# Reading the edge lists and making the chunk tables inside layer 0's front, instead of at the head of the adjacency stage

## The reference, cut to what matters

```python
xn = _layernorm(x, axis=-1)
agg = jax.ops.segment_sum(x[src], dst, num_segments=n)   # inside gin_conv, twice, with src and dst swapped
h = (1.0 + eps) * x + agg
q, k = elu(x @ Wq) + 1, elu(x @ Wk) + 1                  # inside the mix
x = x + gnn(xn, edge_index, ...) + mix(xn[None], ...)[0]
x = x + ffn(_layernorm(x, axis=-1)[None], ...)[0]
```

## Time and profile before

| | |
|---|---|
| median of 3 runs | 2361.12 us (2360.05 to 2365.64) |
| profiled execution, its own time | 2366.88 us |
| its span, first to last instruction | 2365.1 us |
| mean granted TensorE clock | 0.907 of full speed |
| busy: PE, PE weight loads, DVE, ACT, POOL | 1997.1, 1624.9, 1474.2, 1036.3, 551.5 us |

### The profile page before, as it was taken

The page is one execution under the profiler, slowest core; times in us unless marked ns, Lnnn a source line. Parts: engine busy times, 40 slices in busy tenths (PEclk is TensorE's granted clock), DMA queues, the critical chain, the costliest instruction groups (busy, mean ns, idle before and its releaser), DMA issues. The chain is left out here.

```text
span 2365.1 us, 41463 instructions
## 1 busy us (share of the span) xinstructions
PE 1997.1 (84%) x12047; PEld 1624.9 (69%) x12047; DVE 1474.2 (62%) x3791; ACT 1036.3 (44%) x1835; POOL 551.5 (23%) x612
## 2 busy tenths in 40 slices
PE   6938888878877758998697898769999965999998
PEld 3526666656633447998365776569888854999997
DVE  3479999978832655554565322399999656444443
ACT  3525555545511524665351343166666430333332
POOL 1000000047611734554310000000000001454443
PEclk9979999977898559999798999989999956999999
DMA  2014334330077301221502342212121081633332
GB/s 69 0 46 133 117 121 129 109 93 1 1 168 211 103 25 54 71 71 54 127 0 54 95 136 63 56 42 65 53 66 53 0 291 54 195 79 75 49 47 33
DMA packets 90653, 189.74 MB, mean 80 GB/s; under 512 B 14121, under 2 KB 58432, under 8 KB 90570
## 3 DMA queue, kind: packets, MB, share of 16 engines
q1 hardware_dynamic: 72906, 157.31, 23.0%
q0 software_dynamic: 17664, 31.47, 6.4%
HBM read 124.22 MB, written 64.52 MB: 80 GB/s over the span
## 5 line engine op out<-in xcount | busy, mean ns | idle before, releaser
L2224 PEld LDWEIGHTS experts_ps_h<-experts_xt,experts_up 128*128 128x128 f32 x2944 | 351.8, 194 | 10.3 <-issue 3.3
L2224 PE MATMUL experts_ps_h<-experts_xt,experts_up 128*128 128x128 f32 x2944 | 353.0, 277 | 3.0 <-DVE experts_xt L2346 1.8
L2851 PE MATMUL gat_ps_o<-Y,gat_prob_t 125*125 125x256 f32 x1250 | 273.9, 379 | 0.0
L2851 PEld LDWEIGHTS gat_ps_o<-Y,gat_prob_t 125*125 125x125 f32 x1250 | 232.7, 188 | 33.7
L1233 PE MATMUL adj_ps_w<-adj_one_k,adj_one_s 128*125 128x500 bf16 x1000 | 178.8, 305 | 78.6 <-DVE adj_one_k L1164 56.0
L2236 PE MATMUL experts_ps_o<-experts_down,experts_hid 128*128 128x256 f32 x960 | 226.7, 379 | 0.0
L2284 ACT ACTIVATE experts_down<-down 128x1024 f32 (+1 forms) x120 | 138.8, 1157 | 175.7 <-DVE experts_out L2334 77.1
L2316 DVE COPY experts_up<-up 128x1024 f32 (+1 forms) x184 | 123.1, 698 | 112.8 <-issue 68.8
L1233 PEld LDWEIGHTS adj_ps_w<-adj_one_k,adj_one_s 128*125 128x125 bf16 x1000 | 98.3, 138 | 128.6 <-DVE adj_one_k L1164 60.2
L2236 PEld LDWEIGHTS experts_ps_o<-experts_down,experts_hid 128*128 128x128 f32 x960 | 173.2, 190 | 18.7
L1177 ACT ACTIVATE adj_tile<-adj_ps_w 125x500 bf16<-125x500 f32 x250 | 95.8, 438 | 150.1 <-PE adj_ps_w L1233 150.1
(11 more groups left out here) (436 smaller groups left out, 3783.9 us busy)
## 6 DMA issues: line engine op xcount, KB each, us to landing
adjacency<-adj_tile SPq DMA_DIRECT2D x25, 683.6 KB
adjacency_t<-adj_tile_t SPq DMA_DIRECT2D x25, 683.6 KB
adj_in<-adjacency_t SPq DMA_DIRECT2D x25, 683.6 KB
QT<-adjacency SPq DMA_DIRECT2D x25, 683.6 KB
cnt<-adjacency_t SPq DMA_DIRECT2D x25, 683.6 KB
up<-in_L_ffn_w SPq DMA_DIRECT2D x32, 512.0 KB, 6.3
down<-in_L_ffn_w SPq DMA_DIRECT2D x16, 512.0 KB, 7.1
up<-in_L_ffn_W SPq DMA_DIRECT2D x8, 512.0 KB, 6.2
```

The lines of the kernel that those rows point to most:

```text
L2224: last = nc.tensor.matmul(ps[:, h * 128:(h + 1) * 128], w[:, k * H + h * 128:k * H + (h + 1) * 128], xt[b][:, k, :], start=(k == 0), stop= ...
L2851: last = nc.tensor.matmul(ps_o[b][0:ROWS, 0:C], prob_t[:, s * ROWS:(s + 1) * ROWS], K.Y[:, s, :], start=(s == 0), stop=(s == TILES - 1))
```

## The change

The tiles of the lists and tables, and the code that makes them, move from `build_adjacency` into a class `Edges`. Its tiles are allocated ahead of `front`'s and stay through both stages (`MixDown`'s weights are now allocated ahead of them too). `front` of layer 0 calls the pieces: SP loads the three lists behind the rows of group 1 and ahead of `wq`; POOL writes the number rows first, and runs the all-reduce behind the copy of group 3 (`GROUPS - 2`); DVE does seven portions between the tiles of its groups. DVE's and POOL's loops over groups become straight code there. `build_adjacency` keeps the windows alone. `front` of layer 1 has no `edges` and is as it was.

```diff
-def front(nc, K, stage, w_y, y_width, w_kv, w_q, y_scale, x_from=None, x_landed=None, next_sems=0):
+def front(nc, K, stage, w_y, y_width, w_kv, w_q, y_scale, x_from=None, x_landed=None, next_sems=0, edges=None):
...
             rows(1)
+            if edges is not None:
+                edges.load(sp, K.D)
             sp.dma_start(wq[:], w_q.rearrange("(k p) o -> p k o", p=128)).then_inc(w_in, 16)
...
                     if u < 2:
                         then(u)
+                    if edges is not None:
+                        if (g, u) == (0, 3):
+                            edges.widen(dve)
+                        if (g, u) == (1, 2):
+                            edges.halves(dve)
+                        if (g, u) == (1, 3):
+                            edges.keys(dve)
+                        if (g, u) == (2, 2):
+                            edges.presence(dve)
+                        if (g, u) == (2, 3):
+                            edges.spans(dve)
+                        if (g, u) == (3, 3):
+                            edges.bounds(dve)
+                        if (g, u) == (4, 1):
+                            edges.chunks(dve)
...
-            if x_from is not None:
-                with pool.Fori(0, GROUPS) as g:
+            if edges is not None:
+                edges.numbers()
+                for g in range(GROUPS):
                     save(g)
+                    if g == GROUPS - 2:
+                        edges.spread_spans(pool)
...
+    def spread_spans(self, pool):
+        pool.wait_ge(self.span_ready, 1)
+        self.nc.gpsimd.partition_all_reduce(self.span_all[:].rearrange("p a q w -> p (a q w)"),
...
+    def halves(self, dve):
+        v = self.nc.vector
+        v.tensor_scalar(self.off[:], self.src_f[:], 0.5, 1.0 / ROWS, ALU.add, ALU.mult)
+        v.tensor_reduce(self.least[:], self.dst_rows[:], AX.X, ALU.min)
+        dve.drain()
+        v.tensor_copy(self.hi_i[:], self.off[:])
+        v.tensor_reduce(self.most[:], self.dst_rows[:], AX.X, ALU.max)
+        dve.drain()
+        v.tensor_copy(self.hi[:], self.hi_i[:])
+        dve.drain()
...
+    def bounds(self, dve):
+        dve.wait_ge(self.spread, 1)
+        self.nc.vector.tensor_reduce(self.ends[:], self.span_all[0:1].rearrange("p a q w -> p a w q"), AX.X, ALU.max)
+        dve.drain()
```

More of the change, by code:

```diff
@@ L374, in group @@
                 last.then_inc(q_used, 1)
-            overlapped(dve, GROUPS, (statistics, normalise), group)
+            if edges is None:
+                overlapped(dve, GROUPS, (statistics, normalise), group)
+            else:
+                statistics(0, 0)
+                normalise(0, 0)
+                for g in range(GROUPS - 1):
+                    group(g, g % 2, lambda k: (statistics, normalise)[k](g + 1, (g + 1) % 2))
+                group(GROUPS - 1, 0, lambda k: None)
             dve.wait_ge(sum_done, 1 + START)
@@ L967, in build_adjacency @@
         m = Memory(nc, st, "adj", K.banks)
[L968 to L992, removed]
+        E = K.edges
+        low_all, key_all, key_row, win_key, table = E.low_all, E.key_all, E.key_row, E.win_key, E.table
         one_s = [m.sb(f"one_s{i}", (CH, FIXED, ROWS), BF16) for i in range(2)]
@@ L1111, in _ @@
-            v.tensor_reduce(most[:], dst_rows[:], AX.X, ALU.max)
-            dve.wait_ge(made, 1 + START)
-            v.tensor_scalar(rank_up[:], chunk_no[:], 1.0, None, ALU.add)
-            v.tensor_scalar(rank_down[:], chunk_no[:], -1.0, float(CHUNK_ROWS), ALU.mult, ALU.add)
-            dve.drain()
-            for q in range(4):
-                v.tensor_scalar(here[:, q, :], win_first[:], float(WIN - 1), least[:, q:q + 1], ALU.add, ALU.is_ge)
-                v.tensor_scalar(here2[:, q, :], win_first[:], most[:, q:q + 1], None, ALU.is_le)
@@ L1119, in _ @@
-            dve.drain()
-            v.tensor_tensor(here[:], here[:], here2[:], ALU.mult)
-            dve.drain()
-            for q in range(4):
-                v.tensor_scalar(span[:, 0, q, :], here[:, q, :], rank_up[:, q:q + 1], None, ALU.mult)
-                last = v.tensor_scalar(span[:, 1, q, :], here[:, q, :], rank_down[:, q:q + 1], None, ALU.mult)
-            last.then_inc(span_ready, 1)
-            dve.wait_ge(spread, 1 + START)
-            v.tensor_reduce(ends[:], span_all[0:1].rearrange("p a q w -> p a w q"), AX.X, ALU.max)
@@ L1128, in _ @@
-            dve.drain()
-            v.tensor_scalar(row[:, 0, :], ends[:, 1, :], -1.0, float(CHUNK_ROWS), ALU.mult, ALU.add)
-            dve.drain()
-            v.tensor_scalar(row[:, 0, :], row[:, 0, :], float(CHUNKS), None, ALU.min)
-            dve.drain()
-            v.tensor_tensor(row[:, 1, :], ends[:, 0, :], row[:, 0, :], ALU.subtract)
-            dve.drain()
-            v.tensor_copy(table[:, 0:WINS], row[:, 0, :])
-            v.tensor_reduce(most_chunks[:], row[:, 1, :], AX.X, ALU.max)
@@ L2896, in program @@
                     K.QT = sb(conv, "QT0", (128, KC, NODES))
[L2897 to L2898 removed]
                     K.md = MixDown(nc, conv, D)
[L2900 removed]
+                    with ExitStack() as listed:
+                        K.edges = Edges(nc, listed, K.banks)
+                        front(nc, K, "front0", D["L0_gnn_W1_down"], 64, D["L0_mix_Wkv"], D["L0_mix_Wq"], None, D["x"],
+                              next_sems=ADJ_SEMS, edges=K.edges)
+                        build_adjacency(nc, K, D)
                     K.X1 = K.XN
```

137 lines of the change are left out of this document (90 added, 47 removed).

## The result

The changed kernel takes a median of 2341.3 us (2338.24 to 2343.33, 4 runs) against 2361.78 of the kernel before (2360.05 to 2365.64, 4 runs). The ratio on record, from the fast runs, is 0.9907, with an interval from 0.9889 to 0.9926; the two medians by themselves give 0.9913. The forecast was 2341. So the time is right, and so is the large term. Of the small terms three are off, and they offset each other only in part; most of what follows is about these.

A forecast was written before the change was run, and what follows sets the result against it. PE bounds the front, table making alone fills the gap before the windows, and DVE bounds the windows. -23.4 + 3.0 + 0.3 = -20.1 us on the profiled 2366.88 gives 2346.8, a median of about 2341; range 2334 to 2349.

The forecast's parts named there:

- the large term: Between front and first window: table making leaves the path, first window at 130.32 instead of 153.76, -23.4 us.
- The gap: From the front's last DVE copy to the first window: 2.5 us instead of 25.9, so -23.4 us.
- The portions: DVE in the front: 14.9 us of table work over five groups, all hidden in DVE's waits.
- portions not hidden: Rival, DVE in the front: a closer chain through PE and ACT puts 14.9 us back, 2356; chance 0.06.
- The lists: Front's start: 692 KB of transfers ahead of `wq` delay PE's first transposes and the whole front, +3.0 us.
- The queue is full, so the case is nearest the full-share rows: Transfers ahead of `wq`: step choosing +3.0 us, with 217 GB/s giving 3.2 and bounds 0 to 5.2.
- One port: POOL and DVE in the front hold each other up at `halves` or `QT`: 0 to 3.5 us, taken as +0.3.
- POOL's change of code: POOL in group 3, ahead of the all-reduce: 7.2 us, leaving 9.5 us to spare before `bounds`.
- rival on a long change: POOL's code change is long and `bounds` holds the front; slower by over 0.3% from 49 us, 2372 at 60; chance 0.02.
- The entry into the windows: Start of the adjacency stage: taken as free; the rival prices hidden DVE entry at 0 to 5.2 us, chance 0.07.
- The windows at the same pace: Adjacency stage: sign that the windows still take 320 us.
- if a later stage gives time back: Stages behind the adjacency stage: one of the signs that the prediction is wrong.

The follow-up runs named there:

- hold: The changed kernel, but POOL's copy of the normalised rows waits for tile 2's key of the group before; median 2340.74 us, ratio 0.9895 to the kernel before.
- lists: Lists read early as in the changed kernel, but all tables made at the adjacency stage's start and POOL's copies in a loop; median 2360.37 us, ratio 0.9985.
- loop: The changed kernel, but POOL's copies of groups 0 to 3 stand in a loop again, with no new wait; ratio 0.9906.
- shift53: The changed kernel with lists behind all front rows, POOL's copy waiting for tile 2's key, and 53 one-element DVE memsets in the front; ratio 0.9897.
- unrolled: The kernel before, with POOL's loop over its five copies written out and nothing else; ratio 0.9991.

## Why the prediction came out right

**The gap** (-23.4 us) was right to 0.1: the work of the earlier trace rows is gone from the path, and the entry of 2.5 us is all that is left.

**The portions** were hidden, as forecast, in the idle time of DVE that the earlier trace rows shows: the same front of 107.14 us with them (`hold`) and without (`lists`). The working for group 1 was near (tile 3's key by 59.4 at the old times; 60.27 + 0.41 - 0.56 - 0.61 = 59.5 measured, taking off the later start and the 0.61 lost in group 0). The rival "portions not hidden" is refuted.

**The lists** (+3.0 us) were mis-sized: 1.9 us over twelve kernels. The step that failed is "The queue is full, so the case is nearest the full-share rows": a full share was read as a fixed rate, 217 GB/s, while the queue moves up to 348 at the same share, and moved 331 in the old trace. A profile pair is also too little for such a term, since the first transposes scatter by 1.2 to 1.6 us among kernels of one kind.

**One port** (+0.3 us) was mis-sized and put in the wrong place. The forecast looked for new work beside POOL, at `halves` and at `QT`. In the changed kernel neither pair meets: `halves` starts at 57.60, after the copy's end at 57.40, and `QT` at 89.74, after the all-reduce's at 86.84. With the copy behind the key, which the forecast took for granted, the hold-up at `halves` is of the size forecast: `loop` has it, at 0.30 us. The port cost 3.44 us at an old pair, the key of tile 2 and POOL's copy, which the earlier trace rows shows 0.13 us apart, in the order that is good for PE. The forecast named neither that distance nor what writing out both loops does to it. The 3.44 lie just within the stated bound of 3.5. DVE's code without a loop gives 1.05 back, which was not forecast either, so the front grew by 2.39. The Trainium skill, SBUF — State Buffer, "Who interferes with whom", says that whoever issues first gets the shared ports for the whole instruction and the other waits, and that a TENSOR_REDUCE never contends. The trace agrees for POOL's copy: 1.48 us for the key behind a copy of 1.25, 1.40 to 1.52 for the copy behind a key of 0.41, and 0.68 for the reduction beside the copy in `hold`. It doesn't for the all-reduce: the CAST that starts 0.12 us behind it ends at 85.68, 1.16 us ahead of it, and lost 1.59 us, not the 3.11 that were left of it (the spans of such POOL instructions are rough).

**POOL's change of code** was forecast at 7.2 us and took less. In the ten kernels in which the spans are ready before it is over, the all-reduce starts 5.55 to 5.94 us after POOL's last instruction; in the other four it starts 0.14 us after the last span. `bounds` went as forecast, without a wait at 98.87. In the rival on a long change the 2372 is a slip: from slower by 0.3% (2368) at 49 us, each further us lost, 60 us give 2379.

**The entry into the windows** was free, as forecast: in `lists` DVE begins 0.29 us after the front's end. No run shows DVE's entry to be a branch that stalls for a fetch.

**The windows at the same pace** was wrong by 1.8 us, a term the forecast did not have.

In the profiled pair the terms add up to the end of the adjacency stage: -23.46 + 0.56 + 2.39 + 1.82 = -18.69. With 1.9 for the lists it would be -17.4, where -20.1 was forecast and the medians show -20.5. So the forecast was closer than its terms, and that it met the median within 0.3 us is in part luck: it had 1.1 us too much for the lists, 2.1 too little for the port and 1.8 too little for the windows, 2.8 too little in all.

The other 2 or 3 us are not explained. The forecast named "if a later stage gives time back" as a sign of being wrong, and in the profiled pair the stages behind do: from the next stage's first instruction to the end they take 1870.3 us in place of 1880.3. But they are the same code in all fourteen kernels, and in the eleven with the portions in the front they take from 1870.3 (changed) to 1881.2 us (`shift53`), 1875.5 on the mean; `unrolled` takes 1879.8, `lists` 1875.1. So these single executions can't tell a gain of a few us behind from scatter. The interval of the ratio, 17.5 to 26.2 us, leaves it open too.

## What to carry to other kernels

Work that doesn't depend on its neighbours can be put into the idle time of a busy stage at no cost, if it is cut into portions smaller than each idle stretch; read those stretches from the waits of the engine that gets the work, and the wants of the engine that waits for it. But writing out a loop to make room for such portions shifts every instruction in it by hundredths of a microsecond, and where two engines share a port, look up in the old trace which pairs start close to each other (0.13 us here): there such a shift can turn the order, and one wait on the right semaphore fixes it. Put transfers that are needed late behind those that hold the start.

## What was not expected of the hardware

- A distance of 0.05 us decides who has the port: POOL's copy 0.05 us ahead of the key costs PE 0.94 us in groups 1 to 3 (0.61 in group 0), and a copy 0.01 us behind the key costs it nothing.
- Straight code is not simply sooner than a loop: POOL's copy starts 0.06 us after its rows in place of 0.18, DVE's key 0.11 in place of 0.05.
- The transfers moved 209 to 348 GB/s at a share of 1.03 to 1.07.
- POOL's change of code took 5.55 to 5.94 us, and its all-reduce held a CAST for about half of its own length.
- The same loop of DVE ran 317.07 to 319.48 us for 125 windows, by where in DVE's program it lies.
